# Windowed attention layers on one core: the seed of the inverse roots in three two-tensor instructions, and VectorE in place of GpSimd scaling the probabilities

## The chip, the cores and the metric

The kernel runs on one core of one Trainium2 chip. A core has TensorE (PE: matmuls, with a weight load of its own, PEld), VectorE (DVE), ScalarE (ACT), GpSimd (POOL) and SyncE (SP, which here issues the DMAs). The metric is the device time of one execution in microseconds; lower is better.

## The reference, cut to what matters

A small model on 4 x 512 tokens of width 128: a layer norm with a binary feed-forward, an attention with 16 heads, another feed-forward, six "windowed" layers, a recurrent attention, and the same six windowed layers again. The change touches the windowed layers alone. One of them is

```python
q = l2norm(q) * qs                      # over the 64 elements of each of 16 heads
k = l2norm(k) * ksc
q = q * cos * scale + rotate_half(q) * sin * scale
k = k * cos * inv + rotate_half(k) * sin * inv
sim = jnp.einsum('bhwie,bhwje->bhwij', q, k) * 8.0      # windows of 32 queries, 64 keys
attn = jax.nn.softmax(jnp.where(mask, -max, sim), -1)
x = (attn @ v).reshape(b, n, 1024) @ Wo + x
...
xn = (x - mu) / jnp.sqrt(var + 1e-05) * g + bln
a, gate = jnp.split(xn @ W1 + b1, 2, -1)
x = a * gelu(gate) @ W2 + b2 + x
```

The l2norms and the layer norm need inverse square roots. The kernel makes them without a table: a first guess from the bits of the float (a constant less half of the bits read as an integer), and three Newton steps.

## The kernel before, in words

The function `windowed_layers` (called twice) works on tiles of 128 tokens: 4 batch rows of 4 tiles make a layer, 6 layers make 96 tiles, so 192 tiles in all. Each engine walks over the same 105 steps, and in a step it works on tiles of different age: T (projected, squared and rotated now), A (normalised, one step older), B (transposed, and its scores made), C (softmax, and its probabilities times the tokens), D (output projection). The order within a step is written by hand, engine by engine, in the `step` functions of `tensor`, `scalar`, `vector` and `gpsimd`; semaphores alone tie the engines together. There is no scheduler.

The feed-forward of a batch row is spread over the steps that follow its last tile, so that steps come in fours. The names used below: the **up step** (PE `up`, L416; DVE `hidden`, L594, three times), the **down step** (PE L318 multiplies the hidden layer, DVE L615 adds the result to the state ZT, and only then PE L357 subtracts the mean), the **broadcast step** (PE L404, at its end DVE `normal`, L587, makes `xn`), and the **gate step** (PE L411). There are 48 of each.

What VectorE does in a step, in order:

- sum of the probabilities of C (L601) and its reciprocal (L605), once ScalarE's exp (L507) is done
- rotation of the queries of T (L573 and L578, from PSUM into `turned`), once ScalarE has squared them (L478)
- in a down step, the two additions to ZT (L615)
- transpose of C's probabilities into pT (L622), for which PE's `gather` (L288) waits
- the sums of squares of the queries (L582), then the rotation and the sums of squares of the keys
- the seed (L651 to L657): `halved` = -0.5 max(sumsq, 1e-24), the floor itself, the bits shifted right, and their negative plus a constant; 128x36 elements each, once a step
- maximum of B's scores (L661), and scores less the maximum (L667)
- what the feed-forward and the residual need then: L587, the last L594, L679

What GpSimd does in a step: twelve small instructions for the three Newton steps (L713 to L723), the probabilities of C times the reciprocal sums (L740), the sum of the two rotated halves of the queries (L703, `add`), the normalisation of A's queries and keys (L732, twice), and the same sum for the keys (L703 again).

On TensorE a step is: projection of the queries (L252), transposes of B's queries (L258), down product or tokens, output products of D (L296), transposes of B's keys, feed-forward part, projection of the keys (L252), `gather` (L288), feed-forward part, scores (L270, L278).

Of the kernel before, what the change touches and what calls it, by code (L numbers as in the profile page):

```python
# [6 lines left out]
P = 128  # L7
# [3 lines left out]
I32 = mybir.dt.int32  # L11
# [109 lines left out]
def spread(ap, axis, shape):  # L121

    return ap.unsqueeze(axis).broadcast_to(shape)
# [15 lines left out]
def windowed_layers(nc, run, sem, Z, consts, dram):  # L139
# [6 lines left out]
    with ctx:  # L146
# [3 lines left out]
        def ps(name, shape):  # L150
# [16 lines left out]
        bits = sb("bits", [P, NORMS], I32)  # L167
        newton = sb("newton", [P, NORMS])
        halved = sb("halved", [P, NORMS])
        c_1_5 = sb("c_1_5", [P, NORMS])  # L170
        inv_norm = sb("inv_norm", [P, NORMS])
        rstd = sb("rstd", [P, TILES])
        qk = sb("qk", [P, 2, 2, INNER])
# [21 lines left out]
        act_sq, act_tq, act_tk, act_xt = sem("act_sq"), sem("act_tq"), sem("act_tk"), sem("act_xt")  # L195
        act_px, act_exp, act_m = sem("act_px"), sem("act_exp"), sem("act_m")
        act_cen, act_gate, act_gelu = sem("act_cen"), sem("act_gate"), sem("act_gelu")
        dve_turn, dve_ss, dve_floor, dve_shift, dve_guess = [
            sem(s) for s in ("dve_turn", "dve_ss", "dve_floor", "dve_shift", "dve_guess")]
        dve_max, dve_sub, dve_sum, dve_inv, dve_pt = sem("dve_max"), sem("dve_sub"), sem("dve_sum"), sem("dve_inv"), sem("dve_pt")  # L200
        dve_y, dve_var, dve_xn, dve_hid, dve_z, dve_bias = [
            sem(s) for s in ("dve_y", "dve_var", "dve_xn", "dve_hid", "dve_z", "dve_bias")]
        pool_rot, pool_add, pool_newton, pool_inv, pool_qk, pool_p, pool_rstd = [
            sem(s) for s in ("pool_rot", "pool_add", "pool_newton", "pool_inv", "pool_qk", "pool_p", "pool_rstd")]

        ps_qk = ps("ps_qk", [P, 2, 512])
        ps_w = ps("ps_w", [P, 4, 512])
# [350 lines left out]
        def _(dve):  # L558
# [3 lines left out]
            ends = Z[:, EDGE:EDGE + BATCH * SPAN].rearrange("p (b t) -> p b t", b=BATCH)  # L562
            nc.vector.memset(ends[lower, :, SEQ:SPAN], 0.0)
            nc.vector.memset(ends[upper, :, 0:1], 0.0)
            nc.vector.memset(sumsq[:], 1.0).then_inc(edged, 1)
            dve.wait_ge(edged, run + 1)

# [28 lines left out]

            def step(s):
                T, A, B, C, D = s.T, s.A, s.B, s.C, s.D
                if C:
                    dve.wait_ge(act_exp, C.n + 1)  # L600
                    nc.vector.reduce_sum(row_sum[:], probs[:], AXX).then_inc(dve_sum, 1)  # L601
                    dve.wait_ge(dve_sum, C.n + 1)
                    if D:
                        dve.wait_ge(pool_p, C.n)
                    nc.vector.reciprocal(row_inv[:], row_sum[:]).then_inc(dve_inv, 1)  # L605
                if T:
                    if T.k % PER == 0:
                        dve.wait_ge(pool_rot, T.layer + 1)
                    rotate(T, 0)
                if s.down:  # L610
                    f = s.down
                    dve.wait_ge(pe_down, f.m + 1)
# [3 lines left out]
                                                              ALU.add, ALU.add)  # L616
                    last.then_inc(dve_z, 1)
                if C:
                    dve.wait_ge(pool_p, C.n + 1)
                    if D:  # L620
                        dve.wait_ge(pe_px, D.n + 1)
                    nc.vector.transpose(pT[:].rearrange("p a h q -> p h a q"),  # L622
                                        probs[:].rearrange("p h (a k) -> p h a k", a=2)).then_inc(dve_pt, 1)
                if T:
                    sum_squares(T, 0)
                if s.up:
                    hidden(s.up, 0)
# [16 lines left out]
                if s.chain is not None:  # L644
                    if T:
                        dve.wait_ge(dve_ss, T.n * 2 + 2)
                    if s.cen:
                        dve.wait_ge(dve_var, s.cen.m + 1)
                    if s.k:
                        dve.wait_ge(pool_inv, s.chain)  # L650
                    nc.vector.tensor_scalar(halved[:], sumsq[:], 1e-24, -0.5, ALU.max, ALU.mult)  # L651
                    nc.vector.tensor_scalar_max(sumsq[:], sumsq[:], 1e-24).then_inc(dve_floor, 1)
                    dve.wait_ge(dve_floor, s.chain + 1)
                    nc.vector.tensor_scalar(bits[:], sumsq[:].bitcast(I32), 1, None,
                                            ALU.logical_shift_right).then_inc(dve_shift, 1)
                    dve.wait_ge(dve_shift, s.chain + 1)
                    nc.vector.tensor_scalar(bits[:], bits[:], -1.0, float(ROOT_BITS),  # L657
                                            ALU.mult, ALU.add).then_inc(dve_guess, 1)
                if B:
                    dve.wait_ge(pe_s, B.n + 1)  # L660
                    nc.vector.tensor_reduce(neg_max[:], ps_heads, AXX, ALU.max, negate=True).then_inc(dve_max, 1)  # L661
# [24 lines left out]
        def _(pool):  # L686
# [47 lines left out]
            def step(s):  # L734
                T, A, B, C = s.T, s.A, s.B, s.C
                if s.chain_before is not None:
                    invert_roots(s.chain_before, s.bc)
                if C:
                    pool.wait_ge(dve_inv, C.n + 1)
                    nc.gpsimd.tensor_tensor(probs[:], probs[:], spread(row_inv[:], 2, [P, HEADS, KEYS]),  # L740
                                            ALU.mult).then_inc(pool_p, 1)
                if T:
                    add(T, B, 0, pe_tq)
                if A:
                    normalise(A, 0)
                    normalise(A, 1)
                if T:
                    add(T, B, 1, pe_tk)
                if s.k % PER == 6 and s.k // PER + 1 < DEPTH:
                    fold_scale(s.i * 2 + (s.k // PER + 1), (s.k // PER + 1) % 2)  # L750
# [1418 lines left out]
```

## Time and profile before

| | us |
|---|---|
| median of 3 runs | 4568.85 (4562.28 to 4569.06) |
| the profiled execution | 4568.15 |
| its span, first to last instruction | 4566.4 |
| TensorE busy | 4084.1 (89%) |
| VectorE busy | 3362.5 (74%) |
| GpSimd busy | 2758.2 (60%) |
| ScalarE busy | 2061.4 (45%) |

The two sets of windowed layers run from about 575 to 2300 us and from about 2790 to 4530 us. Busy time counts what an instruction's record covers, so a VectorE instruction that has begun and is held up inside the engine counts as busy. Times in the rows below are us from the start of the span; a row of the timeline gives start, length, engine, line, operation, output and inputs, shapes, and in brackets how long the engine had been idle and what ended that.

### The profile page before, as it was taken

The page shows a single profiled execution, that of the slowest core. Times are in us where ns is not written, and L with a number is a line of the kernel's source. Part 1 is how long each engine was busy: PE and PEld are TensorE (multiplying, and loading weights), DVE is VectorE, ACT ScalarE, POOL GpSimd, SP SyncE. Part 2 cuts the span into 40 slices and gives each one's busy share as a digit, 9 for nine tenths or more (in the row PEclk, how much of TensorE's full clock was granted, in tenths as well). Part 3 has the DMA queues.
Part 4 walks back from the last instruction along what each step waited for, and adds up shares of the span by engine and source line. Part 5 has one row for each costly group of instructions (what it writes and reads, how often), then busy time and mean ns, then how long its engine had stood idle before and what let it go on. Part 6 is the DMA issues. An engine that isn't in the chain of part 4 may idle for free. (4 is left out here: it accounts for less than half of the span.)

```text
span 4566.4 us, 129719 instructions
## 1 busy us (share of the span) xinstructions
PE 4084.1 (89%) x55952; PEld 2581.5 (57%) x55952; DVE 3362.5 (74%) x4030; ACT 2061.4 (45%) x2406; POOL 2758.2 (60%) x3511
## 2 busy tenths in 40 slices
PE   8999879999999999999867776899999999999996
PEld 3333346666666666666536663666666566666563
DVE  1575178888888888888634335888888888888883
ACT  2455235555545555555421112455455554554552
POOL 0000078787877777777514214878777777787772
PEclk9899989999999999999976557999999999999997
DMA  0000010000000000000000001000000000000000
GB/s 17 1 1 1 2 55 11 11 16 11 2 17 11 16 11 2 7 2 2 2 7 4 4 4 56 11 11 2 16 11 16 12 2 16 11 7 2 2 2 10
DMA packets 14121, 46.29 MB, mean 10 GB/s; under 512 B 3809, under 2 KB 6241, under 8 KB 11745
## 3 DMA queue, kind: packets, MB, share of 16 engines
q1 hardware_dynamic: 13536, 37.83, 2.4%
q8 instruction: 448, 7.34, 0.7%
q14 instruction: 137, 1.11, 0.1%
HBM read 36.78 MB, written 1.05 MB: 8 GB/s over the span
## 5 line engine op out<-in xcount | busy, mean ns | idle before, releaser
L703 POOL TENSOR_TENSOR w_qk<-w_turned 128x1024 f32<-128x1024 f32 x384 | 906.6, 2361 | 147.8 <-DVE w_turned L578 146.2
L252 PE MATMUL w_ps_qk<-w_w_qk,ZT 128*128 128x512 f32 x1536 | 763.0, 620 | 81.5 <-DVE w_turned L578 53.8
L296 PE MATMUL w_ps_y<-w_px,w_w_vo 128*128 128x128 f32 x6144 | 787.2, 276 | 4.5 <-DVE ZT L679 4.5
L296 PEld LDWEIGHTS w_ps_y<-w_px,w_w_vo 128*128 128x128 f32 x6144 | 742.9, 192 | 79.0 <-issue 75.1
L478 ACT ACTIVATE w_squares<-w_ps_qk 128x1024 f32<-128x1024 f32 x384 | 393.4, 1024 | 777.6 <-PE w_ps_qk L252 776.5
L732 POOL TENSOR_TENSOR w_qk<-w_qk,w_inv_norm 128x1024 f32<-128x1024 f32 x384 | 722.9, 1904 | 0.0
L573 DVE TENSOR_TENSOR w_turned<-w_ps_qk,w_rot_l 128x1024 f32<-128x1024 f32 x384 | 467.3, 1217 | 235.5 <-ACT w_squares L478 209.6
L740 POOL TENSOR_TENSOR w_probs<-w_probs,w_row_inv 128x1024 f32<-128x1024 f32 x192 | 365.6, 1904 | 326.9 <-DVE w_row_inv L605 326.1
L252 PEld LDWEIGHTS w_ps_qk<-w_w_qk,ZT 128*128 128x128 f32 x1536 | 280.5, 195 | 413.5 <-issue 316.6
L482 ACT ACTIVATE w_px<-w_ps_w 128x1024 f32<-128x1024 f32 x384 | 379.2, 1021 | 199.7 <-PE w_ps_w L288 199.7
L578 DVE TENSOR_TENSOR w_turned<-w_ps_qk,w_rot_l 128x1024 f32<-128x1024 f32 x384 | 465.9, 1213 | 0.0
L582 DVE TENSOR_REDUCE w_sumsq<-w_squares 128x16 f32<-128x1024 f32 x384 | 458.0, 1193 | 0.0
L258 PEld LDWEIGHTS w_ps_w<-ident,w_qk 128*128 128x128 f32 x3072 | 352.2, 142 | 139.8 <-issue 137.5
L258 PE MATMUL w_ps_w<-ident,w_qk 128*128 128x128 f32 x3072 | 403.5, 275 | 30.6 <-ACT w_qT L512 29.8
L288 PE MATMUL w_ps_w<-w_pT,w_x_tok 32*128 32x512 f32 x3072 | 389.0, 621 | 13.4 <-issue 8.3
L864 POOL MEMSET n_sel<- 128x512 f32 x6 | 3.2, 527 | 654.4 <-POOLq L1053 308.0
L519 ACT ACTIVATE w_kT<-w_ps_w 128x1024 f32<-128x1024 f32 x192 | 196.7, 1024 | 381.9 <-PE w_ps_w L258 381.9
L601 DVE TENSOR_REDUCE w_row_sum<-w_probs 128x16 f32<-128x1024 f32 x192 | 234.2, 1220 | 176.8 <-ACT w_probs L507 175.6
L278 PE MATMUL w_ps_w<-w_kT,w_qT 64*32 64x64 f32 x24576 | 290.7, 225 | 34.1 <-issue 34.1
L278 PEld LDWEIGHTS w_ps_w<-w_kT,w_qT 64*32 64x32 f32 x24576 | 255.4, 105 | 114.4 <-issue 114.4
L651 DVE TENSOR_SCALAR w_halved<-w_sumsq 128x36 f32<-128x36 f32 x196 | 281.3, 1435 | 7.0
L288 PEld LDWEIGHTS w_ps_w<-w_pT,w_x_tok 32*128 32x128 f32 x3072 | 140.5, 186 | 246.6 <-issue 245.1
(250 smaller groups left out, 6371.0 us busy)
## 6 DMA issues: line engine op xcount, KB each, us to landing
w_w_qk<-in_w_qk SPq DMA_DIRECT2D x12, 1024.0 KB, 4.8
w_w_vT<-in_w_vT SPq DMA_DIRECT2D x12, 512.0 KB, 3.9
w_w_o<-in_w_o SPq DMA_DIRECT2D x12, 512.0 KB, 5.1
w_w<-in_w SPq DMA_DIRECT2D x12, 384.0 KB, 3.1
w_w<-in_w SPq DMA_DIRECT2D x12, 192.0 KB, 3.1
XT<-in_x SPq DMA_DIRECT2D x1, 1024.0 KB, 4.8
w_rot<-in_rot SPq DMA_DIRECT2D x2, 512.0 KB, 5.8
out<-XT SPq DMA_DIRECT2D x1, 1024.0 KB, 3.9
```

The costliest lines, as they stand in the source:

```text
L252: last = nc.tensor.matmul(ps_qk[:, c, :], Z[:, T.col:T.col + P], w_qk[:, T.parity, cols], start=True, stop=True)
L258: last = nc.tensor.transpose(ps_t[:, p // 4, (p % 4) * P:(p % 4 + 1) * P], qk[:, B.odd, which, p * P:(p + 1) * P], ident[:])
L278: last = nc.tensor.matmul(ps_heads[w * WIN:(w + 1) * WIN, h * PAIRS + p, :], qT[rows, p, w * WIN:(w + 1) * WIN], kT[rows, p, col:col + KEY ...
L288: last = nc.tensor.matmul(ps_w[:, w, :], x_tok[rows, C.t, half, :], pT[rows, half].rearrange("p h q -> p (h q)"), start=half == 0, stop=ha ...
L296: last = nc.tensor.matmul(ps_y[:, D.t * P:(D.t + 1) * P].rearrange("p (w q) -> p w q", q=WIN), w_vo[:, D.parity, h, p, :], px[:, D.odd, :, ...
L478: nc.scalar.activation(squares[:, which, :], flat(ps_qk[:]), ACT.Square).then_inc(act_sq, 1)
L482: nc.scalar.activation(px[:, C.odd, pair].rearrange("p w h q -> p (w h q)"), flat(ps_w[:, pair, :]), ACT.Copy).then_inc(act_px, 1)
L573: nc.vector.tensor_tensor(turned[:, which, 0, :].rearrange("p (h d) -> p h d", d=DH), flat(ps_qk[:]).rearrange("p (h d) -> p h d", d=DH), ...
L578: nc.vector.tensor_tensor(turned[:, which, 1, :].rearrange("p (h two d) -> p h two d", two=2, d=HALF), swapped, sin, ALU.mult).then_inc(dv ...
L582: nc.vector.reduce_sum(sumsq[:, which * HEADS:(which + 1) * HEADS], squares[:, which, :] .rearrange("p (h d) -> p h d", d=DH), AXX).then_i ...
L703: nc.gpsimd.tensor_tensor(qk[:, T.odd, which, :], turned[:, which, 0, :], turned[:, which, 1, :], ALU.add).then_inc(pool_add, 1)
L732: nc.gpsimd.tensor_tensor(heads, heads, spread(inv, 2, [P, HEADS, DH]), ALU.mult).then_inc(pool_qk, 1)
```

## The change

Three edits, all in `windowed_layers`.

The seed: `halved` and the floored sums came from two instructions with one tensor and two constants each, the guess from two more. Now there are three `scalar_tensor_tensor` instructions, each with two tensors as inputs: the floor (both inputs are `sumsq`), the guess (the bits times -0.5 plus a tile that holds the constant), and `halved` (times -0.5 plus a tile of zeros). The two constant tiles are set once per set of layers.

The probabilities: the multiplication by the reciprocal sums leaves GpSimd and becomes a VectorE `tensor_tensor` right behind the reciprocal. The semaphore `pool_p` becomes `dve_p`.

The order on VectorE: the queries of T are rotated first in a step, ahead of the sums of C.

```diff
             def step(s):
                 T, A, B, C, D = s.T, s.A, s.B, s.C, s.D
+                if T:
+                    if T.k % PER == 0:
+                        dve.wait_ge(pool_rot, T.layer + 1)
+                    rotate(T, 0)
                 if C:
                     dve.wait_ge(act_exp, C.n + 1)
                     nc.vector.reduce_sum(row_sum[:], probs[:], AXX).then_inc(dve_sum, 1)
                     dve.wait_ge(dve_sum, C.n + 1)
-                    if D:
-                        dve.wait_ge(pool_p, C.n)
                     nc.vector.reciprocal(row_inv[:], row_sum[:]).then_inc(dve_inv, 1)
-                if T:
-                    if T.k % PER == 0:
-                        dve.wait_ge(pool_rot, T.layer + 1)
-                    rotate(T, 0)
+                    dve.wait_ge(dve_inv, C.n + 1)
+                    nc.vector.tensor_tensor(probs[:], probs[:], spread(row_inv[:], 2, [P, HEADS, KEYS]),
+                                            ALU.mult).then_inc(dve_p, 1)
...
                 if C:
-                    dve.wait_ge(pool_p, C.n + 1)
+                    dve.wait_ge(dve_p, C.n + 1)
...
                 if T:
+                    if s.chain_before is not None:
+                        dve.wait_ge(dve_guess, s.chain_before + 1)
                     sum_squares(T, 0)
...
-                    nc.vector.tensor_scalar(halved[:], sumsq[:], 1e-24, -0.5, ALU.max, ALU.mult)
-                    nc.vector.tensor_scalar_max(sumsq[:], sumsq[:], 1e-24).then_inc(dve_floor, 1)
+                    nc.vector.scalar_tensor_tensor(sumsq[:], sumsq[:], 1e-24, sumsq[:], ALU.max, ALU.max).then_inc(dve_floor, 1)
                     dve.wait_ge(dve_floor, s.chain + 1)
-                    nc.vector.tensor_scalar(bits[:], sumsq[:].bitcast(I32), 1, None,
-                                            ALU.logical_shift_right).then_inc(dve_shift, 1)
-                    dve.wait_ge(dve_shift, s.chain + 1)
-                    nc.vector.tensor_scalar(bits[:], bits[:], -1.0, float(ROOT_BITS),
-                                            ALU.mult, ALU.add).then_inc(dve_guess, 1)
+                    nc.vector.scalar_tensor_tensor(bits[:], sumsq[:].bitcast(I32), -0.5, c_seed[:], ALU.mult, ALU.add)
+                    nc.vector.scalar_tensor_tensor(halved[:], sumsq[:], -0.5, c_zero[:], ALU.mult,
+                                                   ALU.add).then_inc(dve_guess, 1)
...
                 if s.chain_before is not None:
                     invert_roots(s.chain_before, s.bc)
-                if C:
-                    pool.wait_ge(dve_inv, C.n + 1)
-                    nc.gpsimd.tensor_tensor(probs[:], probs[:], spread(row_inv[:], 2, [P, HEADS, KEYS]),
-                                            ALU.mult).then_inc(pool_p, 1)
                 if T:
                     add(T, B, 0, pe_tq)
```

How the rows stand on the engines. VectorE in a down step, from the residual (L679) to the transpose of the probabilities, before:

```order
L679 TENSOR_TENSOR ZT<-w_ps_y,ZT 64x512 x2
L601 TENSOR_REDUCE w_row_sum<-w_probs 128x16
L605 RECIPROCAL w_row_inv<-w_row_sum 128x16
L569 ISA
L571 REGISTER_ALU
L573 TENSOR_TENSOR w_turned<-w_ps_qk,w_rot_l 128x1024
L578 TENSOR_TENSOR w_turned<-w_ps_qk,w_rot_l 128x1024
L615 SCALAR_TENSOR_TENSOR ZT<-w_ps_f,w_vec,ZT 64x512 x2
L622 STREAM_TRANSPOSE w_pT<-w_probs 128x16x2x32
```

The same place of the changed kernel (its lines are numbered up to four higher):

```order
L680 TENSOR_TENSOR ZT<-w_ps_y,ZT 64x512 x2
L570 ISA
L572 REGISTER_ALU
L574 TENSOR_TENSOR w_turned<-w_ps_qk,w_rot_l 128x1024
L579 TENSOR_TENSOR w_turned<-w_ps_qk,w_rot_l 128x1024
L606 TENSOR_REDUCE w_row_sum<-w_probs 128x16
L608 RECIPROCAL w_row_inv<-w_row_sum 128x16
L610 TENSOR_TENSOR w_probs<-w_probs,w_row_inv 128x1024
L617 SCALAR_TENSOR_TENSOR ZT<-w_ps_f,w_vec,ZT 64x512 x2
L624 STREAM_TRANSPOSE w_pT<-w_probs 128x16x2x32
```

The rotation has moved ahead of the sums, and a multiplication of 128x1024 stands ahead of the additions to ZT and of the transpose.

GpSimd between the last Newton step and the next guess, before:

```order
L717 TENSOR_TENSOR w_newton<-w_newton,w_c_5 128x36
L723 TENSOR_TENSOR w_inv_norm<-w_newton,w_inv_norm 128x36
L740 TENSOR_TENSOR w_probs<-w_probs,w_row_inv 128x1024
L703 TENSOR_TENSOR w_qk<-w_turned 128x1024
L732 TENSOR_TENSOR w_qk<-w_qk,w_inv_norm 128x1024 x2
L703 TENSOR_TENSOR w_qk<-w_turned 128x1024
```

And in the changed kernel:

```order
L718 TENSOR_TENSOR w_newton<-w_newton,w_c_5 128x36
L724 TENSOR_TENSOR w_inv_norm<-w_newton,w_inv_norm 128x36
L704 TENSOR_TENSOR w_qk<-w_turned 128x1024
L733 TENSOR_TENSOR w_qk<-w_qk,w_inv_norm 128x1024 x2
L704 TENSOR_TENSOR w_qk<-w_turned 128x1024
```

One of five large instructions is gone, and the sum of the rotated queries is the first thing behind the Newton steps.

## Rows read from the trace of the kernel before

**Rows 1.** The page, busy time of each engine over the whole span.
```profile
PE 4084.1 (89%) x55952; PEld 2581.5 (57%) x55952; DVE 3362.5 (74%) x4030; ACT 2061.4 (45%) x2406; POOL 2758.2 (60%) x3511
```
**Rows 2.** Busy time by stretch (header: engines, clock, DMA), inside the windowed layers.
```profile
1400.00:2200.00 800.00, 752.97 (x9901) 498.49 (x9899) 699.65 (x798) 420.28 (x478) 625.39 (x807) 1.00 0.02 6
```
**Rows 3.** Waits: who waited for whom, total us, times, longest.
```profile
PE w_ps_f L318 <- DVE w_hid L594: 51.2, 40, 3.0
PE w_ps_f L265 <- DVE w_xn L587: 38.1, 31, 1.6
PE w_ps_f L357 <- DVE ZT L615: 15.6, 43, 1.6
...
PE w_ps_w L288 <- DVE w_pT L622: 5.1, 2, 2.6
```
**Rows 4.** Groups by line: busy us, mean ns of one, idle before.
```profile
L740 POOL TENSOR_TENSOR w_probs<-w_probs,w_row_inv 128x1024 f32<-128x1024 f32 x192 | 365.6, 1904 | 326.9 <-DVE w_row_inv L605 326.1
L651 DVE TENSOR_SCALAR w_halved<-w_sumsq 128x36 f32<-128x36 f32 x196 | 281.3, 1435 | 7.0
...
L615 DVE SCALAR_TENSOR_TENSOR ZT<-w_ps_f,w_vec,ZT 64x512 f32<-64x512 f32 x96 | 71.6, 746 | 16.8 <-PE w_ps_f L318 16.0
```
**Rows 5.** Timeline of VectorE in one down step.
```profile
1612.53 1.39 DVE L679 TENSOR_TENSOR ZT<-w_ps_y,ZT 64x512 f32<-64x512 f32 x2
1613.95 1.22 DVE L601 TENSOR_REDUCE w_row_sum<-w_probs 128x16 f32<-128x1024 f32 x1
1615.20 0.25 DVE L605 RECIPROCAL w_row_inv<-w_row_sum 128x16 f32<-128x16 f32 x1
1615.48 1.23 DVE L573 TENSOR_TENSOR w_turned<-w_ps_qk,w_rot_l 128x1024 f32<-128x1024 f32 x1
1616.62 1.22 DVE L578 TENSOR_TENSOR w_turned<-w_ps_qk,w_rot_l 128x1024 f32<-128x1024 f32 x1
1617.76 1.51 DVE L615 SCALAR_TENSOR_TENSOR ZT<-w_ps_f,w_vec,ZT 64x512 f32<-64x512 f32 x2
1619.29 1.25 DVE L622 STREAM_TRANSPOSE w_pT<-w_probs 128x1024 f32<-128x1024 f32 x1
```
**Rows 6.** Timeline of TensorE in the same down step.
```profile
1619.32 1.13 PE L357 MATMUL w_ps_f<-ZT,centre 128*128 128x512 f32 x2 [0.25 <-DVE ZT L615]
```
**Rows 7.** Timeline of VectorE in one up step.
```profile
1669.10 1.23 DVE L622 STREAM_TRANSPOSE w_pT<-w_probs 128x1024 f32<-128x1024 f32 x1
1670.26 1.18 DVE L582 TENSOR_REDUCE w_sumsq<-w_squares 128x16 f32<-128x1024 f32 x1
1671.43 0.75 DVE L594 SCALAR_TENSOR_TENSOR w_hid<-w_ps_f,w_b_h,w_hid 128x512 f32<-128x512 f32 x1
1672.31 1.23 DVE L573 TENSOR_TENSOR w_turned<-w_ps_qk,w_rot_l 128x1024 f32<-128x1024 f32 x1
...
1676.48 1.24 DVE L651 TENSOR_SCALAR w_halved<-w_sumsq 128x36 f32<-128x36 f32 x1
...
1678.06 0.18 DVE L657 TENSOR_SCALAR w_bits<-w_bits 128x36 int32<-128x36 int32 x1
```
**Rows 8.** Timeline of ScalarE, TensorE and GpSimd in the same up step.
```profile
1663.37 1.03 ACT L478 ACTIVATE w_squares<-w_ps_qk 128x1024 f32<-128x1024 f32 x1 [1.11 <-PE w_ps_qk L252]
...
1671.15 2.00 PE L288 MATMUL w_ps_w<-w_pT,w_x_tok 32*128 32x512 f32 x16
...
1675.31 2.37 POOL L703 TENSOR_TENSOR w_qk<-w_turned 128x1024 f32<-128x1024 f32 x1
```
**Rows 9.** Recurrent attention: timeline of GpSimd and VectorE, then L1901's durations (min/median/max).
```profile
2494.08 2.13 POOL L2039 TENSOR_TENSOR a_wkbT<-a_rkT,a_E 128x512 f32<-128x512 f32 x2
...
2494.27 2.03 DVE L1901 SCALAR_TENSOR_TENSOR a_S<-a_S,a_total,a_kv 128x64 f32<-128x64 f32 x2
...
L1901 DVE SCALAR_TENSOR_TENSOR a_S<-a_S,a_total,a_kv x56: 276/283/1296, 2482.3 to 2753.8; 128x64 f32<-128x64 f32 x56
```
**Rows 10.** Timeline of TensorE in one gate step: the tokens wait for xn.
```profile
1648.19 0.44 PE L265 MATMUL w_ps_f<-ident,ZT 128*128 128x128 f32 x2 [1.62 <-DVE w_xn L587]
```

More of the change, by code:

```diff
@@ L169, in windowed_layers @@
         halved = sb("halved", [P, NORMS])
-        c_1_5 = sb("c_1_5", [P, NORMS])
+        c_1_5, c_zero, c_seed = sb("c_1_5", [P, NORMS]), sb("c_zero", [P, NORMS]), sb("c_seed", [P, NORMS])
         inv_norm = sb("inv_norm", [P, NORMS])
@@ L197, in windowed_layers @@
         act_cen, act_gate, act_gelu = sem("act_cen"), sem("act_gate"), sem("act_gelu")
-        dve_turn, dve_ss, dve_floor, dve_shift, dve_guess = [
-            sem(s) for s in ("dve_turn", "dve_ss", "dve_floor", "dve_shift", "dve_guess")]
-        dve_max, dve_sub, dve_sum, dve_inv, dve_pt = sem("dve_max"), sem("dve_sub"), sem("dve_sum"), sem("dve_inv"), sem("dve_pt")
+        dve_turn, dve_ss, dve_floor, dve_guess = [sem(s) for s in ("dve_turn", "dve_ss", "dve_floor", "dve_guess")]
+        dve_max, dve_sub, dve_sum, dve_inv, dve_pt, dve_p = sem("dve_max"), sem("dve_sub"), sem("dve_sum"), sem("dve_inv"), sem("dve_pt"), sem("dve_p")
         dve_y, dve_var, dve_xn, dve_hid, dve_z, dve_bias = [
             sem(s) for s in ("dve_y", "dve_var", "dve_xn", "dve_hid", "dve_z", "dve_bias")]
-        pool_rot, pool_add, pool_newton, pool_inv, pool_qk, pool_p, pool_rstd = [
-            sem(s) for s in ("pool_rot", "pool_add", "pool_newton", "pool_inv", "pool_qk", "pool_p", "pool_rstd")]
+        pool_rot, pool_add, pool_newton, pool_inv, pool_qk, pool_rstd = [
+            sem(s) for s in ("pool_rot", "pool_add", "pool_newton", "pool_inv", "pool_qk", "pool_rstd")]
         ps_qk = ps("ps_qk", [P, 2, 512])
@@ L564, in _ @@
             nc.vector.memset(ends[upper, :, 0:1], 0.0)
+            nc.vector.memset(c_zero[:], 0.0)
+            nc.vector.memset(c_seed[:], float(ROOT_BITS))
             nc.vector.memset(sumsq[:], 1.0).then_inc(edged, 1)
```

## The prediction, made before the changed kernel was run

> **What bounds the kernel now.** I read the page's busy shares first, then busy time by stretch, the waits of TensorE, and last the timelines of two steps. Over the whole span TensorE is busy 89% and VectorE 74% [rows 1]. Inside the windowed layers it is closer: of 800 us TensorE is busy 753 (94%) at full clock, VectorE 700 (87%), GpSimd 625 (78%) [rows 2]. So TensorE bounds the layers, and what it still loses it loses to VectorE: in front of the down product 51.2 us in 40 of 48 down steps, in front of the tokens of the gate step 38.1, in front of the mean (L357) 15.6 in 43 steps [rows 3]. Before `gather` it lost only 5.1 us, in two places [rows 3], so the transposed probabilities have been early. The reader should see that VectorE is both the nearly full engine and the one waited for: what lengthens its chain at one of these points lengthens the kernel.
>
> VectorE's own stalls are hidden in its busy time. L651 works on 36 elements and takes 1435 ns on average [rows 4]. In the up step it runs from 1676.48 to 1677.72, and the GpSimd sum L703 from 1675.31 to 1677.68 [rows 7, 8]: it ends 0.04 us behind GpSimd, so it was held until GpSimd let go of something. That is the stall which the new seed seems to avoid, so what holds what is the main question.
>
> **The seed.** Does an instruction with two tensors in SBUF escape? The trace before has such a one: L1901 (a_S and a_kv, 64 elements). Its median is 283 ns; two of them, beside two GpSimd sums (L2039, 2494.08 to 2496.21), took 2.03 us together and ended at 2496.30, 0.09 behind the second sum, and the longest of the 56 took 1296 [rows 9]. So two tensors wait for GpSimd as one did. I cost the first of the three instructions at the same stall as L651: it ends about 0.04 behind the end of L703. Behind that point the old seed takes 1677.72 to 1678.24, 0.52 us [rows 7]. For the two instructions left, each lies between L657's 0.18 and L1901's 0.28 [rows 7, 9], near 0.22, with a wait of 0.03: about 0.5. Bounds: 0.4 to 0.6, a change of -0.1 to +0.1 a step. I take nothing. The seed ends when L703 of the keys ends, as before.
>
> The Trainium skill speaks against this edit too. Its page "SBUF — State Buffer", section "Who interferes with whom", says that a VectorE instruction with two SBUF inputs contends with a GpSimd instruction that reads SBUF, just as one in a two-port mode does, and that whichever comes second blocks entirely; by its page "VectorE: DVE Perf Modes", section "Mode 2×_2P — use both read ports for one tensor", leaving `tensor_scalar` would have left the two-port mode. By that rule the seed gains nothing; by the rule that only the mode matters it would gain the whole stall (a rival below). Rows 9 side with the first.
>
> **The multiplication on VectorE.** It takes GpSimd's 192 instructions of 1904 ns away [rows 4]; GpSimd waited for the reciprocal sums anyway (326.1 us), so that is worth nothing by itself. On VectorE 128x1024 elements take 1.23 us (L573 [rows 5]). Its inputs, probabilities and reciprocals, both lie in SBUF, so it waits for GpSimd like L1901. And it comes at a bad moment: GpSimd's sum of the rotated queries starts when the rotation (L578, in the new order the first work of a step) is done, lasts 2.37, and the multiplication is ready 1.45 later, after the sum of 1.22 and the reciprocal of 0.25 [rows 5, 8]. It is held for about 1.0 and ends about 1.1 behind the end of L703: an estimate from the short ones, which ended 0.04 and 0.09 behind GpSimd with lengths of about 0.18 and 0.28, so some 0.15 less than their length. Bounds: not held at all, or held to the end of L703 and then its full 1.23.
>
> **Down step, on the path that sets the end.** From L679's end, 1613.92, as before [rows 5]. New: rotation 1613.95 to 1616.30 (2.36 as in rows 5), sum to 1617.44, reciprocal to 1617.72, multiplication ready at 1617.75. GpSimd's sum starts about 0.08 behind the rotation, 1616.39, and ends at 1618.75; multiplication to 1619.85; L615 twice, 1.51 less 0.08 of overlap, to 1621.28. Before it ended at 1619.27, and L357 started at 1619.32, having waited [rows 5, 6]. So TensorE goes on 2.0 us later, and everything behind it too. Of these 2.0, 1.2 is the multiplication, and most of the rest the hold.
>
> **Up step.** Here the rotation is free to start at 1664.43, when the squares are made (1663.37 plus 1.03 [rows 8]). Rotation to 1666.79, sum to 1667.92, reciprocal to 1668.20; GpSimd's sum 1666.87 to 1669.24; multiplication to 1670.34; transpose to 1671.60 (before 1670.33). `gather` started at 1671.15 with 0.8 us to spare [rows 7, 8]; it now starts 0.5 late. Sum of squares to 1672.70, L594 to 1673.37, rotation of the keys to 1675.65, against 1674.66 before (1672.31 plus 2.35). GpSimd's sum for the keys then starts at 1675.73 instead of 1675.31 and ends 0.42 later, and the seed, the maximum, the subtraction and the last L594, for which the down product waits, with it: +0.4. The 0.5 at `gather` does not add to it, since the down product waited anyway (1.28 us on average) [rows 3].
>
> **Broadcast and gate step.** By the same working the transposed probabilities end 1.25 later, and `gather` is 0.4 late in the broadcast step. The tokens of the gate step then wait 1.62 us for xn [rows 10], which hides that: xn hangs on the GpSimd sum for the keys, which here is set by GpSimd's own queue, and that queue is shorter. In the gate step `gather` is about 0.1 late. Together +0.1, bounds 0 and +0.6.
>
> **Sum.** 2.0 + 0.4 + 0.1 = 2.5 us for each group of four steps. L615 has 96 instructions, two for each, so 48 groups [rows 4]: 48 x 2.54 = 122 us. Against the profiled execution's 4568.15, which lies 0.7 below the median of the runs, that gives 4690. The new wait ahead of the query's sum of squares is for an instruction of the same engine long done: nothing. The memsets are four in all: nothing.
>
> **Rivals.**
>
> *Two-tensor instructions are not held* (faster). Then the seed loses its stall and the multiplication costs 1.23 alone. Down step: multiplication 1617.75 to 1618.98, L615 to 1620.41, +1.1. Up step: rotation of the keys +0.1, but the seed ends 0.9 earlier than before. Broadcast step: xn up to 1.1 earlier, all of which the 1.62 us wait gives back. Together -0.9 a group, 48 x -0.9 = -43: 4525. It decides if the seed's first instruction no longer ends with GpSimd's L703. For it: no large `tensor_tensor` with two SBUF inputs ran beside GpSimd in this trace. Against it: rows 9. Chance 0.11.
>
> *The multiplication is not held, the seed is.* Down step +1.1, up step -0.3, xn earlier by 0.55: +0.3 a group, 4568 + 14 = 4582. For it: one is a `tensor_tensor` with a repeated operand, L1901 is not. Against it: both read two tensors of SBUF. Chance 0.08.
>
> *GpSimd keeps what it holds over its whole queue* (slower still). Then the multiplication waits behind one normalisation or both, 1.9 or 3.8 us more in each of 192 steps, of which next to nothing is hidden: 4690 + 365 = 5055, or more. Against it: both L1901 of rows 9 took 2.03 us beside two GpSimd sums back to back, so the first got in between them. Chance 0.04.
>
> The forecast itself keeps 0.77. Within it, a hold shorter by 0.4 in the down step takes off 20 us, an overlap that I don't see (the fetch of TensorE's instructions, layers without a wait) perhaps 20 more; the upper bounds (full 1.23, seed +0.1, broadcast and gate 0.6) add 35. So its own range is 4650 to 4727. The range given reaches down to the second rival and a little further.
>
> **Chances.** What a measurement of this kernel tells from no change is about 0.2%, 9 us. Faster: the first rival and a little of the second, 0.12. Within 0.2%: a part of the second, 0.05. Slower: the rest, 0.83.
>
> **What would show it.** Right: the new multiplication's mean near 2.2 us instead of 1.23, ending 1.1 behind GpSimd's first sum of a step; the first seed instruction near 1.2 to 1.5 us mean with the other two near 0.2; TensorE's wait before L357 near 2 us in all 48 down steps, and waits before `gather` of about 0.5 in most up and broadcast steps; VectorE above 90% busy in the layers. Wrong: a multiplication of 1.23 us throughout (a rival), a first seed instruction of 0.2 us (the first rival), or a wait before L357 that stays near 0.3 us.

## The result and the profile after

The changed kernel is slower.

| | before | changed |
|---|---|---|
| median, us | 4567.8 (4562.28 to 4569.06, 4 runs) | 4751.01 (4741.71 to 4754.46, 4 runs) |
| ratio, 95% interval | | 1.040 (1.0382 to 1.0418) |
| the profiled execution, us | 4568.15 | 4741.71 |
| its span, us | 4566.4 | 4739.5 |

That is 183 us by the medians and 174 by the profiled executions, where 122 were forecast. The sign was right, the size was not: 4751 lies above the range's upper end, 4735. (The median before has one run more in it than the one that stood ahead of the prediction, 4568.85.)

Busy time over the whole span, and then in 800 us inside the windowed layers (PE, PEld, DVE, ACT, POOL, granted clock), of the changed kernel:

```profile
PE 4118.0 (87%) x55952; PEld 2617.5 (55%) x55952; DVE 3677.3 (78%) x4030; ACT 2048.4 (43%) x2406; POOL 2577.6 (54%) x3319
```
```profile
1400.00:2200.00 800.00, 720.21 (x9258) 475.64 (x9260) 728.93 (x749) 393.77 (x451) 549.98 (x712) 0.98 0.02 7
```

Against [rows 1, 2]: in the layers TensorE went from 753 to 720 us of 800, VectorE from 700 to 729, so VectorE is now the busier one. TensorE's busy time over the whole span rose by 34 us although it runs the same 55952 matmuls, and its granted clock in this stretch is 0.98 instead of 1.00. Nothing in the prediction made room for a change of the clock; it turns out to be the term that was left out.

Groups of instructions by line (busy us, mean ns), changed kernel:

```profile
L610 DVE TENSOR_TENSOR w_probs<-w_probs,w_row_inv 128x1024 f32<-128x1024 f32 x192 | 407.4, 2122 | 6.6
L655 DVE SCALAR_TENSOR_TENSOR w_sumsq<-w_sumsq 128x36 f32<-128x36 f32 x196 | 225.5, 1150 | 6.8
L657 DVE SCALAR_TENSOR_TENSOR w_bits<-w_sumsq,w_c_seed 128x36 int32<-128x36 int32 x196 | 42.9, 219 | 6.8
L733 POOL TENSOR_TENSOR w_qk<-w_qk,w_inv_norm 128x1024 f32<-128x1024 f32 x384 | 905.2, 2376 | 0.2
L356 PE MATMUL w_ps_f<-ZT,centre 128*128 128x512 f32 x96 | 63.7, 750 | 95.4 <-DVE ZT L617 95.4
```

The multiplication takes 2122 ns where its work takes some 1.2 us, and the first instruction of the new seed takes 1150 on 36 elements: both are held, as the old L651 was [rows 4]. GpSimd pays too: its normalisations rose from 1904 to 2376 ns on average. The matmul of the mean (L357 before, L356 now) takes 750 ns instead of 640.

Who waited for whom on TensorE (total us, times, longest), changed kernel:

```profile
PE w_ps_w L287 <- DVE w_pT L624: 162.5, 148, 3.0
PE w_ps_f L356 <- DVE ZT L617: 95.4, 45, 2.6
PE w_ps_w L277 <- issue: 38.2, 30, 2.0
PE w_ps_f L317 <- DVE w_hid L595: 32.7, 40, 2.5
```

Against [rows 3]: the wait before `gather` went from 5.1 to 162.5 us, the one before the mean from 15.6 to 95.4, and the one before the down product fell from 51.2 to 32.7. Three more waits fell: for the rotated queries from 53.8 to 17.2, before the tokens from 38.1 to 14.2, before the transposes (L258, now L257) from 29.8 to 14.1.

One down step of the changed kernel, VectorE, then GpSimd, then TensorE:

```profile
1522.67 1.23 DVE L574 TENSOR_TENSOR w_turned<-w_ps_qk,w_rot_l 128x1024 f32<-128x1024 f32 x1
1523.82 1.22 DVE L579 TENSOR_TENSOR w_turned<-w_ps_qk,w_rot_l 128x1024 f32<-128x1024 f32 x1
1524.95 1.21 DVE L606 TENSOR_REDUCE w_row_sum<-w_probs 128x16 f32<-128x1024 f32 x1
1526.19 0.25 DVE L608 RECIPROCAL w_row_inv<-w_row_sum 128x16 f32<-128x16 f32 x1
1526.48 2.07 DVE L610 TENSOR_TENSOR w_probs<-w_probs,w_row_inv 128x1024 f32<-128x1024 f32 x1
1528.47 1.50 DVE L617 SCALAR_TENSOR_TENSOR ZT<-w_ps_f,w_vec,ZT 64x512 f32<-64x512 f32 x2
1530.01 1.25 DVE L624 STREAM_TRANSPOSE w_pT<-w_probs 128x1024 f32<-128x1024 f32 x1
```
```profile
1525.11 2.36 POOL L704 TENSOR_TENSOR w_qk<-w_turned 128x1024 f32<-128x1024 f32 x1 [2.87 <-DVE w_turned L579]
1527.43 4.74 POOL L733 TENSOR_TENSOR w_qk<-w_qk,w_inv_norm 128x1024 f32<-128x1024 f32 x2
```
```profile
1521.40 2.84 PE L317 MATMUL w_ps_f<-w_hid,w_w 128*128 128x512 f32 x6 [0.79 <-DVE w_hid L595]
...
1530.03 1.13 PE L356 MATMUL w_ps_f<-ZT,centre 128*128 128x512 f32 x2 [2.24 <-DVE ZT L617]
1531.00 1.88 PE L251 MATMUL w_ps_qk<-w_w_qk,ZT 128*128 128x512 f32 x4
```

This is the walk of the prediction. GpSimd's sum starts 0.07 us behind the rotation and ends at 1527.47; the multiplication, ready at 1526.48, ends at 1528.55, 1.08 behind it (1.1 was taken, and 1.08 is also the median over the kernel's 192 multiplications); ZT ends at 1529.97, and the mean starts 8.63 behind the down product where it started 6.65 behind it before (1619.32 [rows 6], less 1612.67, when L318 started): 2.0 later, as worked out. The two normalisations took 4.74 us where a pair takes 3.8: while VectorE multiplies, GpSimd is held in turn.

The same three matmul groups in another down step, and then the clock in both places (last three numbers of a row: granted clock, DMA share, GB/s), changed kernel:

```profile
1604.40 1.73 PE L356 MATMUL w_ps_f<-ZT,centre 128*128 128x512 f32 x2 [2.24 <-DVE ZT L617]
1605.92 3.02 PE L251 MATMUL w_ps_qk<-w_w_qk,ZT 128*128 128x512 f32 x4
```
```profile
1604.30:1608.90 4.60, 4.50 (x10) 1.68 (x10) 2.39 (x3) 1.08 (x2) 2.23 (x2) 0.63 0.46 129
1529.90:1532.90 3.00, 2.87 (x10) 1.15 (x10) 2.42 (x3) 1.08 (x2) 2.27 (x2) 1.00 0.00 0
```

Both steps wait 2.24 us, and in this one the mean then takes 1.73 instead of 1.13 and the keys 3.02 instead of 1.88 us: about 1.7 us more, at a granted clock of 0.63, so mostly at 1.2 instead of 2.4 GHz. The clock fell behind the wait in one case and not in the other. From the start of the `gather` of an up step to that of the next down step, 22 of 44 have no stretch of the lower level in them and take 21.2 us (median); the other 22 take 22.8.

Between the first mean of a set of layers and its last but one, the clock records of the changed kernel have 33 stretches at the lower level, 119 us together, and those of the kernel before have 4, 17 us together. Of the 33, 31 begin between 0.3 us before and 1.4 us behind the end of a wait of 1.8 to 2.7 us: 18 at the wait for ZT, 10 at the one before `gather`, 3 at the one before the scores (L277). The wait for ZT was over 1.8 us in 39 of the 48 down steps, so the lower level followed it in about half of them. The Trainium skill (page "TensorE: Matmul & The Clock Gate", section "Part 1: The HAM clock gate") says that the throttled state is the default and activity releases it; these rows agree, in that the lower level follows a wait (31 of the 33).

### The profile page after: what moved, and what is told of

It is laid out like the page before. It is cut to its first block and busy times, and to the rows that moved or that the text cites. A ratio compares the mean times of both kernels' runs of the same rounds, so it can differ in the third digit from the quotient of the medians.

```text
span 4739.5 us, 129151 instructions
## 1 busy us (share of the span) xinstructions
PE 4118.0 (87%) x55952; PEld 2617.5 (55%) x55952; DVE 3677.3 (78%) x4030; ACT 2048.4 (43%) x2406; POOL 2577.6 (54%) x3319
## 5 line engine op out<-in xcount | busy, mean ns | idle before, releaser
L704 POOL TENSOR_TENSOR w_qk<-w_turned 128x1024 f32<-128x1024 f32 x384 | 906.4, 2360 | 810.6 <-DVE w_turned L579 734.3
L733 POOL TENSOR_TENSOR w_qk<-w_qk,w_inv_norm 128x1024 f32<-128x1024 f32 x384 | 905.2, 2376 | 0.2
L251 PE MATMUL w_ps_qk<-w_w_qk,ZT 128*128 128x512 f32 x1536 | 775.8, 630 | 41.5 <-DVE w_turned L579 17.2
L574 DVE TENSOR_TENSOR w_turned<-w_ps_qk,w_rot_l 128x1024 f32<-128x1024 f32 x384 | 468.5, 1220 | 232.7 <-ACT w_squares L477 211.3
L287 PE MATMUL w_ps_w<-w_pT,w_x_tok 32*128 32x512 f32 x3072 | 403.8, 640 | 169.4 <-DVE w_pT L624 162.5
L251 PEld LDWEIGHTS w_ps_qk<-w_w_qk,ZT 128*128 128x128 f32 x1536 | 293.4, 200 | 364.4 <-issue 339.5
L257 PEld LDWEIGHTS w_ps_w<-ident,w_qk 128*128 128x128 f32 x3072 | 353.8, 142 | 121.6 <-issue 121.4
L257 PE MATMUL w_ps_w<-ident,w_qk 128*128 128x128 f32 x3072 | 403.8, 275 | 14.9 <-ACT w_qT L511 14.1
L610 DVE TENSOR_TENSOR w_probs<-w_probs,w_row_inv 128x1024 f32<-128x1024 f32 x192 | 407.4, 2122 | 6.6
L287 PEld LDWEIGHTS w_ps_w<-w_pT,w_x_tok 32*128 32x128 f32 x3072 | 157.6, 191 | 407.9 <-issue 406.7
L277 PE MATMUL w_ps_w<-w_kT,w_qT 64*32 64x64 f32 x24576 | 291.7, 225 | 38.2 <-issue 38.2
L277 PEld LDWEIGHTS w_ps_w<-w_kT,w_qT 64*32 64x32 f32 x24576 | 255.8, 105 | 120.4 <-issue 120.4
L662 DVE TENSOR_REDUCE w_neg_max<-w_ps_w 128x16 f32<-128x1024 f32 x192 | 234.1, 1219 | 71.5 <-PE w_ps_w L277 70.1
L668 DVE TENSOR_TENSOR w_probs<-w_ps_w,w_neg_max 128x1024 f32<-128x1024 f32 x192 | 235.2, 1225 | 20.5 <-DVE w_neg_max L662 0.9
```

Of the source, the lines that this page charges most:

```text
L251: last = nc.tensor.matmul(ps_qk[:, c, :], Z[:, T.col:T.col + P], w_qk[:, T.parity, cols], start=True, stop=True)
L257: last = nc.tensor.transpose(ps_t[:, p // 4, (p % 4) * P:(p % 4 + 1) * P], qk[:, B.odd, which, p * P:(p + 1) * P], ident[:])
L277: last = nc.tensor.matmul(ps_heads[w * WIN:(w + 1) * WIN, h * PAIRS + p, :], qT[rows, p, w * WIN:(w + 1) * WIN], kT[rows, p, col:col + KEY ...
L287: last = nc.tensor.matmul(ps_w[:, w, :], x_tok[rows, C.t, half, :], pT[rows, half].rearrange("p h q -> p (h q)"), start=half == 0, stop=ha ...
L574: nc.vector.tensor_tensor(turned[:, which, 0, :].rearrange("p (h d) -> p h d", d=DH), flat(ps_qk[:]).rearrange("p (h d) -> p h d", d=DH), ...
L610: nc.vector.tensor_tensor(probs[:], probs[:], spread(row_inv[:], 2, [P, HEADS, KEYS]), ALU.mult).then_inc(dve_p, 1)
```

## The experiments

All ratios are to runs of the kernel before on the same chip. Three questions: what holds the multiplication, what the clock is worth, and which part of the change does what.

### The new seed alone

Kernel before, with the new seed and its wait, and nothing else of the change:

```diff
-                    nc.vector.tensor_scalar(halved[:], sumsq[:], 1e-24, -0.5, ALU.max, ALU.mult)
-                    nc.vector.tensor_scalar_max(sumsq[:], sumsq[:], 1e-24).then_inc(dve_floor, 1)
+                    nc.vector.scalar_tensor_tensor(sumsq[:], sumsq[:], 1e-24, sumsq[:], ALU.max, ALU.max).then_inc(dve_floor, 1)
...
```

> The kernel before with the new seed alone (three two-tensor instructions, and the wait ahead of the sum of squares). Theory 1, two SBUF inputs are held by GpSimd just as the old form was: the first seed instruction keeps a mean of 1.2 to 1.5 us, time within 10 us of before (4558 to 4578). Rival, the new form is not held: the first instruction takes 0.2 us, and the time falls by 40 us or more (under 4530).

Measured 4559.54 us, ratio 0.9978 (0.9968 to 0.9988). The first instruction:

```profile
L655 DVE SCALAR_TENSOR_TENSOR w_sumsq<-w_sumsq 128x36 f32<-128x36 f32 x196 | 284.2, 1450 | 6.8
```

It is held like L651 (1450 against 1435 ns [rows 4]), and the rival (0.2 us, under 4530) falls. The seed is worth about 10 us (5 to 15 by the interval), a little more than the nothing that was taken.

### The multiplication alone, in the old order

```diff
                     nc.vector.reciprocal(row_inv[:], row_sum[:]).then_inc(dve_inv, 1)
+                    dve.wait_ge(dve_inv, C.n + 1)
+                    nc.vector.tensor_tensor(probs[:], probs[:], spread(row_inv[:], 2, [P, HEADS, KEYS]),
+                                            ALU.mult).then_inc(dve_p, 1)
                 if T:
...
                     rotate(T, 0)
```

> The kernel before with the multiplication moved to VectorE, behind the reciprocal, but with the rotation of the queries still behind it, and the old seed. GpSimd then has no large instruction in hand when the multiplication is ready. Theory 1 (held by GpSimd, as a matter of place): the multiplication takes 1.23 to 1.3 us instead of 2.12, TensorE waits before the mean of the down step about 1.3 us instead of 2.1, and before gather about as much as in the changed kernel (the transpose ends as late, 1.25 later than before); 4670 to 4710, so slower than before but 40 us or more faster than the change. Rival (a multiplication of two SBUF tensors is slow in itself, 2.1 us): mean 2.1, and no better than the change, 4750.

Measured 4825.49 us, ratio 1.0564 (1.0540 to 1.0588). The instruction itself behaved as theory 1 says: 1245 ns, at a place where GpSimd has nothing large in hand. The time did not: 4670 to 4710 was expected, and it is the slowest of all. TensorE now waits for the rotated queries, 53.8 us before and 204.2 here:

```profile
PE w_ps_qk L252 <- DVE w_turned L578: 204.2, 153, 2.7
PE w_ps_f L357 <- DVE ZT L616: 68.5, 45, 1.8
```

I had priced the place of the multiplication for the transpose and ZT and forgotten that the rotation behind it had no slack. Its clock records have 28 stretches at the lower level, counted as above.

### The new order alone

```diff
                 if T:
...
                     rotate(T, 0)
                 if C:
                     dve.wait_ge(act_exp, C.n + 1)
...
-                    rotate(T, 0)
```

> The kernel before with the new order alone: queries rotated ahead of the sums, GpSimd still scales the probabilities. Theory A: the wait of TensorE for the rotated queries (53.8 us) shrinks to under 20, but GpSimd scales the probabilities later in the down step, not earlier, and its sum of the queries now may stand in front; the transposed probabilities come 0.5 to 2 us later and gather waits: 4560 to 4620. Theory B: the reorder is the part that gains and the rest of the change only hides it: 4530 to 4550.

Measured 4678.45 us, ratio 1.0236 (1.0217 to 1.0254): slower than even theory A gave it. With the probabilities still scaled by GpSimd, the transpose now stands right behind the sums and waits 338.1 us for GpSimd (11.2 us idle before):

```profile
L622 DVE STREAM_TRANSPOSE w_pT<-w_probs 128x1024 f32<-128x1024 f32 x192 | 239.1, 1245 | 338.1 <-POOL w_probs L740 338.1
```

So the two edits do not add up: the order alone costs 2.4%, the place of the multiplication alone 5.6%, and the change, which has both and the seed, 4.0%. Once the multiplication is on VectorE the new order helps (5.6 to 4.0%); with the multiplication on GpSimd it hurts.

### The second input from PSUM

```diff
-                    nc.vector.tensor_tensor(probs[:], probs[:], spread(row_inv[:], 2, [P, HEADS, KEYS]),
-                                            ALU.mult).then_inc(dve_p, 1)
+                    nc.vector.tensor_tensor(probs[:], probs[:], ps_heads[:, :, 0:1].broadcast_to([P, HEADS, KEYS]),
+                                            ALU.max).then_inc(dve_p, 1)
```

> The changed kernel with the second input of the multiplication read from PSUM (a column of the scores that lie there, repeated) instead of SBUF, and the maximum of the two in place of the product, so the softmax is left without its normalisation; all else the same. Theory 1 (two SBUF inputs are what is held): the instruction takes 1.23 us in every step instead of a mean of 2.12, the wait before the mean falls from 2.1 to about 1.2 us, the wait before gather nearly vanishes, 4570 to 4610. Rival (any VectorE instruction that writes SBUF beside GpSimd, or this instruction's shape, is slow): 2.1 us and 4750.

Measured 4536.86 us, ratio 0.9930 (0.9910 to 0.9950): 4.7 points under the change, and faster than the kernel before. (A point is one per cent of the time before.) Two things differ in the instruction, where the second operand lies and the operation, and its output is not the reference's softmax; the version further below with the reciprocals in PSUM keeps the multiplication and settles which of the two it is.

```profile
L610 DVE TENSOR_TENSOR w_probs<-w_probs,w_ps_w 128x1024 f32<-128x1024 f32 x192 | 234.3, 1220 | 6.6
```
```profile
PE w_ps_f L356 <- DVE ZT L617: 59.2, 44, 1.6
PE w_ps_f L317 <- DVE w_hid L595: 35.7, 41, 2.6
PE w_ps_w L287 <- DVE w_pT L624: 33.1, 24, 1.8
```

1220 ns in place of 2122, and the wait before `gather` 33 instead of 162 us. GpSimd's normalisations are back at 1905 ns as well. So the hold needs both inputs in SBUF. The time went below the 4570 to 4610 that I gave.

### TensorE kept busy in the wait for ZT

The changed kernel, with two matmuls more in the wait (they ran in 42 of the 48 down steps):

```diff
                 if s.cen:
+                    if s.down and s.T and s.C:
+                        pe.wait_ge(dve_sub, s.C.n + 1)
+                        for _ in range(2):
+                            nc.tensor.matmul(ps_s[:, 0, :], ident[:], w_qk[:, s.T.parity, 0:512],
+                                             start=True, stop=True, skip_group_check=True)
```

> The changed kernel with two extra fp32 matmuls of 128x512 in front of the mean of each down step, into a part of PSUM that nobody reads; they need nothing that is late, and lie in the 2.2 us for which TensorE waits for ZT. They add about 1.9 us of work a step that only fills the wait. Theory 2 (part of the loss that the prediction left out is TensorE's clock, which the trace grants at 1.2 instead of 2.4 GHz in a stretch behind many of these waits: the down steps with it last 22.6 us, those without 21.0): the 22.6 us steps become 21.0, about 20 of 48, and the time falls by 20 to 40 us, to 4710 to 4730, in spite of the added work. Rival (the clock has another cause, or the steps differ for another reason): no fall, 4745 to 4770.

Measured 4702.22 us, ratio 1.0285 (1.0266 to 1.0304) against 1.040 for the change: 49 us less by the medians, 0.0115 x 4568 = 52 by the ratios and 42 by the profiled executions, by adding work to the engine that bounds the kernel.

```profile
L354 PE MATMUL w_ps_w<-w_w_qk,ident 128*128 128x512 f32 x168 | 79.1, 593 | 0.0
...
L361 PE MATMUL w_ps_f<-ZT,centre 128*128 128x512 f32 x96 | 53.8, 643 | 25.6 <-DVE ZT L622 25.6
```

The mean is back at 643 ns (750 in the change, 640 before), and the clock records have 11 stretches at the lower level, counted as above, where the change has 33; none of them follows the wait for ZT any more. The waits before `gather`, which this run leaves alone, are still 163.0 us in all, and 8 of the 11 stretches follow one of them. The fall was larger than the 20 to 40 us expected.

Could the fill have helped in another way than by the clock? The traces say no. I took the time from one mean (L356; L357 before, L361 here) to the next, which is one group of four steps, over the first 23 means of each set of layers, so 44 groups (us; a group counts as free when no stretch of the lower clock touches it):

| | before | changed | wait filled |
|---|---|---|---|
| groups free of the lower clock | 41 | 17 | 33 |
| mean length of those | 69.5 | 72.3 | 72.3 |
| all 44 together | 3071 | 3243 | 3208 |
| 44 times the mean of the free ones | 3060 | 3183 | 3183 |
| difference, the part of the clock | 11 | 60 | 25 |

At full clock the filled kernel is as long as the changed one, so all of what it gains in these groups (36 us) is clock. And of the 172 us by which the 44 groups of the changed kernel are longer than before, 49 go with the clock and 123 are there without it.

### The keys ahead of the mean

In the changed kernel, and the same edit in the kernel before:

```diff
                 if s.cen:
+                    if s.down and s.T:
+                        pe.wait_ge(dve_turn, s.T.n * 2 + 1)
+                        project(s.T, 1, pe_k)
...
-                if T:
+                if T and not (s.cen and s.down):
                     pe.wait_ge(dve_turn, T.n * 2 + 1)
                     project(T, 1, pe_k)
```

and on ScalarE the squares of the keys ahead of those of the centred rows.

> The changed kernel with the projection of the keys (TensorE) and their squares (ScalarE) put ahead of the mean in the down step. The wait for ZT is then filled with work that has to be done anyway. Theory (the held multiplication costs what it costs because ZT ends on the path, and the keys behind it): the mean starts where it did, gather about 1.5 us earlier, and the stretches at half clock in the down steps go: 48 x 1.5 + 30 = 100 us less, 4640 to 4670. Rival (something else in the step is late at once, the transpose of the probabilities or the seed): 4700 to 4745.

> The kernel before with the keys ahead of the mean in the down step, as above. There TensorE waits for ZT only 0.3 us a step (15.6 us in all). Expected from that: 10 to 25 us less, 4540 to 4557; the rotation of the keys starts about 1.2 us earlier, which helps only where VectorE is late afterwards. Rival: none of it reaches the end, 4560 to 4570.

Measured in the changed kernel 4659.16 us, ratio 1.0190 (1.0173 to 1.0207), as expected: the wait for ZT hides work that has to be done anyway, and 12 stretches at the lower clock are left of 33. In the kernel before 4543.83 us, ratio 0.9944 (0.9927 to 0.9961), a gain of about 25 us, at the upper end of what was expected.

### GpSimd's sum behind the multiplication

```diff
+                if C:
+                    pool.wait_ge(dve_p, C.n + 1)
                 if T:
                     add(T, B, 0, pe_tq)
```

> The changed kernel, but GpSimd starts its sum of the rotated queries only when VectorE has finished the multiplication. No instruction is left out or added. Theory 1: the multiplication takes 1.23 to 1.3 us instead of 2.12; GpSimd's queue starts 2.7 us later in each step, for which it has room (it waits 810 us for rotated queries and keys), so nearly all of the gain of the run with the PSUM operand comes, less where GpSimd's sum of the keys then starts late: 4540 to 4600. Rival (GpSimd has no room, its queue becomes what the seed waits for): 4650 and more.

Measured 4623.74 us, ratio 1.0112 (1.0095 to 1.0129). The multiplication is free (1225 ns), with both inputs in SBUF as in the change: so the hold also needs GpSimd to have something in hand. But the gain is 127 us and not the 214 of the PSUM operand, halfway to the rival: GpSimd did not have the room that its idle time seemed to promise. Its sum of the keys starts 0.89 us behind the rotation of the keys (median; 0.08 in the change), since its own queue is late; the seed ends 3.65 us behind that rotation instead of 2.83, and the down product and the tokens wait longer (32.7 and 14.2 us in the change):

```profile
PE w_ps_f L317 <- DVE w_hid L595: 61.8, 39, 3.2
...
PE w_ps_f L264 <- DVE w_xn L588: 46.9, 36, 1.9
```

### Versions that use this

The reciprocal sums kept in PSUM, in 16 columns of the score banks that are free between the subtraction and `gather`:

```diff
-        row_inv = sb("row_inv", [P, HEADS])
+        row_inv = ps_s[:, 0, 0:HEADS]
```

> The changed kernel with the reciprocal sums written to and read from PSUM (16 columns of the score banks, free at that time); it computes the whole reference. The multiplication then has one input in SBUF. Theory 1: as in the run with the PSUM operand, 1.22 us and 4530 to 4550, so faster than before. Rival (writing PSUM and reading it back costs, or the score banks are not free so early): 4560 or more.

Measured 4529.62 us, ratio 0.9922 (0.9906 to 0.9939), at the lower end of what was expected. The multiplication is a multiplication here, with one input in PSUM, and takes 1221 ns; the reciprocal, which now writes PSUM, takes 261 ns instead of 253:

```profile
L610 DVE TENSOR_TENSOR w_probs<-w_probs,w_ps_w 128x1024 f32<-128x1024 f32 x192 | 234.4, 1221 | 6.7
```

So it was the place of the operand and not the operation.

The same with the keys ahead of the mean:

> The same, and the projection of the keys ahead of the mean in the down step. What TensorE still waits for ZT (59.2 us with the PSUM operand) is then filled: 40 to 60 us less than the run before, 4480 to 4500. Rival (VectorE is the bound by then, at over 85% busy, and the waits come back before the down product or gather): 4510 to 4540.

Measured 4471.80 us, ratio 0.9794 (0.9777 to 0.9810): 58 us less than the run before, as expected.

The kernel before with the new seed and the keys first:

> The kernel before with the new seed and the keys ahead of the mean, the multiplication left on GpSimd. The two gains measured apart (0.2% and 0.6%) add up: 4530 to 4545. Rival: they overlap, both only making the seed end earlier, 4545 to 4560.

Measured 4529.54 us, ratio 0.9920 (0.9903 to 0.9936): the two small gains add up.

And the version with PSUM and keys first, where GpSimd starts its sum of the keys behind VectorE's guess:

```diff
                 if T:
+                    pool.wait_ge(dve_guess, s.chain + 1)
                     add(T, B, 1, pe_tk)
```

> The second of this set (reciprocals in PSUM, keys first), and GpSimd starts its sum of the rotated keys only behind VectorE's guess. Nothing is left out. Theory 1 for the seed (two SBUF inputs are held as well): its first instruction falls from a mean of 1.2 us to 0.2, the seed ends 1.0 to 1.2 us earlier in each step, and the waits before the down product and the tokens shrink: 20 to 50 us less than the run before. Rival (the first seed instruction is slow for another reason): it stays at 1.2 us and the time rises, since GpSimd's queue starts later.

Measured 4449.45 us, ratio 0.9748 (0.9725 to 0.9772), the fastest of all, 22 us less than the run before. The first instruction of the seed without this wait and with it:

```profile
L660 DVE SCALAR_TENSOR_TENSOR w_sumsq<-w_sumsq 128x36 f32<-128x36 f32 x196 | 224.9, 1147 | 6.8
```
```profile
L660 DVE SCALAR_TENSOR_TENSOR w_sumsq<-w_sumsq 128x36 f32<-128x36 f32 x196 | 40.7, 208 | 6.8
```

1147 ns become 208 with the same instruction, and the wait before the down product falls from 34.2 to 17.8 us. TensorE is busy 767.89 of 800 us in the layers in this version.

## Why the prediction was too small

**The held seed: right.** The two-tensor form is held as the old one was (1450 ns alone, 1150 in the change). Moving GpSimd's sum away frees it (208), so it is GpSimd that holds it.

**The held multiplication: right in kind and in length.** A mean of 2122 ns (2.2 forecast), ending 1.08 us behind GpSimd's sum (1.1). The operand in PSUM and the delayed sum each free it, to 1220 and 1225. The rival in which GpSimd keeps what it holds over its whole queue falls with it, since the multiplication ends before GpSimd's next instruction does.

**The rival in which the multiplication is not held: falls.** Its time was wrong as well: 4582 forecast, 4537 measured with the operand in PSUM. Which of its terms was off was not separated by a run. So the hold costs 214 us (4751 less 4537) where the prediction had 108 between the two. Part of the 214 is the clock: with the operand in PSUM 3 stretches at the lower level are left of 33. And the change without it would have been one of 0.7% to the good.

**The down step: right.** In the step shown ZT ends 2.0 us later, as worked out; the wait before the mean is 95.4 us in 45 steps. VectorE is 91% busy in the layers, as forecast.

**The steps with `gather`: too small.** In the up step the rotation of the queries starts at 1504.22, and the transpose ends 7.15 us behind it, as in the working (7.17):

```profile
1510.12 1.25 DVE L624 STREAM_TRANSPOSE w_pT<-w_probs 128x1024 f32<-128x1024 f32 x1
```
```profile
1508.75 1.88 PE L251 MATMUL w_ps_qk<-w_w_qk,ZT 128*128 128x512 f32 x4
1511.62 2.00 PE L287 MATMUL w_ps_w<-w_pT,w_x_tok 32*128 32x512 f32 x16 [0.99 <-DVE w_pT L624]
```

But TensorE waits 0.99 us there where 0.5 was forecast. `gather` starts 0.25 us behind the end of the transpose, where I took 0.05 from the mean, and TensorE arrives earlier, since other waits have shrunk. Part of the 162.5 us before `gather` is thus only moved; how much is new loss no run separates.

**The step that failed: "TensorE goes on 2.0 us later, and everything behind it too."** That sentence prices a longer wait at its length, and the sum had no term for TensorE's clock, which so stood at nothing without a reason. The new waits took the clock from 2.4 to 1.2 GHz in 33 stretches where there had been 4, and about 1.6 us went with it in each of 22 down steps. By the 44 groups of the table the clock cost 49 us, and filling the wait gave back 42 to 52. The rest of the growth, 2.8 us a group at full clock, is near the 2.54 of the forecast: 123 us over the 44 groups where it gives 112.

**Luck in that 2.54.** At full clock the hold costs more than forecast, and what else is in the change costs less. Groups free of the lower clock last 69.1 us with the operand in PSUM, so the hold is worth 3.3 us a group (2.2 between the forecast and the second rival), and the rest of the change -0.5 (+0.3 forecast). The two errors nearly cancel. The upper end of the prediction's own range is a slip as well: 4690 and 35 are 4725, not 4727.

**What would have been the right read.** The stretch in [rows 2] has a granted clock of 1.00, but longer waits were to be had elsewhere in the trace before: the longest in front of the down product is 3.0 us [rows 3]. Two waits of that length, and the stretch of the first (the last three numbers are granted clock, DMA share, GB/s), kernel before:

```profile
2234.41 4.27 PE L318 MATMUL w_ps_f<-w_hid,w_w 128*128 128x512 f32 x6 [2.99 <-DVE w_hid L594]
...
4460.67 2.84 PE L318 MATMUL w_ps_f<-w_hid,w_w 128*128 128x512 f32 x6 [2.98 <-DVE w_hid L594]
```
```profile
2234.40:2238.70 4.30, 4.29 (x8) 0.66 0.00 0
```

One came with the lower clock, at a cost of 1.4 us (4.27 less 2.84), and the other did not; DMA traffic, which was there in the slow down step shown above (0.46), has no part in this one (0.00). So the price of the new wait had to be given as a range: its length, and up to 1.4 us more in each of the 48 down steps, 67 us. That is 4690 to 4757, which holds 4751. How many of the steps would pay could not be read from the trace before.

## What to carry to other kernels

- Before work moves to VectorE beside a busy GpSimd, look where its inputs lie and what GpSimd has in hand when it starts. Here an instruction with two inputs in SBUF was held until GpSimd's sum had ended, and then held GpSimd's next one; one input in PSUM (even 16 columns, repeated) or another order of starts took that away, worth 4.8 and 2.9 points.
- A new wait of the engine that bounds the kernel is priced at its length and, if it is longer than what the engine had there before, at up to a stretch of half clock behind it (here in 22 of 44 down steps). Work moved into the wait gains twice.
- Two edits on the same chain of work do not add up (2.4 and 5.6% alone, 4.0% together). Judge them in the pair, and look for what had no slack (here the rotated queries).

## What was not expected of the hardware

- The same wait of 2.24 us was followed by the lower clock in one down step and not in another. Adding 79.1 us of matmuls to the bounding engine made the kernel about 50 us faster.
- VectorE gets in between two GpSimd instructions that stand back to back: the multiplication ended 1.08 us behind L704 although GpSimd's L733 was next, and the pair of L733 took 4.74 instead of 3.8 us (2 x 1904 ns).
- GpSimd idle for 810.6 us in front of its sums still had too little room for a start that is 2.7 us later a step: moving it gained 127 us, the operand in PSUM 214.
